# The last stage of a two-layer decoder: its weights loaded and split inside the stage before, its rows finished batch by batch

## Chip, cores and metric

One core of a Trainium2 chip runs the whole program in one launch. The metric is the device time of an execution in microseconds (us), lower is better.

## What is computed

The reference is a decoder of two layers on 8 sequences (batches) of 128 tokens with 512 features, every part followed by a residual add and a layernorm. The change touches the last two parts, a cross attention and a linear layer with routed low-rank adapters:

```python
x = _layernorm(x + _L1_xattn_ref(x, ctx, mask, Wq, Wk, Wv, Wo, q_norm_w, k_norm_w))   # 32 heads, 8 kv groups of 4, head size 128
q = x[:, 107:-1, :].mean(axis=1)
routing = softmax(q @ router_W.T + router_b)          # 8 experts
base = x @ W.T + b                                    # W: 512 x 512
t = einsum('bsd,erd->bser', x, A)                     # A: 8 experts x 16, 512
lora = einsum('bser,eor,be->bso', t, B, routing) * 2.0
x = _layernorm(x + base + lora)
```

All float32. A matmul to near float32 accuracy is made of three products in the type fp32r: each operand is split into a rounded high part and the low part left over, and high x high, low x high and high x low are accumulated (`three`, lines 69 to 73).

## The kernel before

`program` (line 2078) runs six stages one after the other. A stage owns its buffers, PSUM banks and semaphores; each engine has its own instruction stream in a stage, written out by hand, and engines meet only at semaphores. Between stages the semaphores are cleared and all engines meet at a barrier (lines 2096, 2097). No planner orders anything: the order of an engine's work is the order of the code. `m` holds what lives through all stages: x by token (`xtok`, token on the partition, batch, feature), x transposed and split (`xT_hi`, `xT_lo`), the context likewise, and small arrays of the layernorm.

**The second cross attention** (`cross1_stage`, line 873) works in 64 units, 8 groups of heads times 8 batches, unit u = 8 * group + batch. Its weights come group by group: SyncE loads raw q, k and v, and o weights (lines 912 to 930), each when the split of the group before has freed the raw buffer; GpSimd splits the next group while TensorE works on this one. A piece of the split is two GpSimd operations, a product with ones that gives the high part (line 937) and a subtract (line 939). A group has 2 pieces for k and v, 4 for q and 4 for o, spread over the eight steps of the group (lines 977 to 984): k and v in steps 0 and 1, q in steps 1 to 4, o in steps 4 to 7. In the same stream GpSimd multiplies the probabilities (line 972), takes the powers to -1/2 for the layernorm of finished batches (`batch_rstd`, line 1583, called from 976) and those of the q and k norm (line 989), which VectorE waits for in each unit. While the last group is worked on (units 56 to 63), the code before has nothing to split, and the layernorm of the stage runs batch by batch, from step 60 on: `batch_stats` (1572 to 1578) and `batch_scale` (1588) on VectorE, transposes on TensorE (1595), the split of the transposed x on ScalarE and VectorE (1601, 1606).

**The last stage** (`lora_stage`, line 1950). SyncE issues six loads: router weights and bias, the bias of the layer, A, W and B (lines 1982 to 1987). VectorE sums the high and low parts of x over the tokens 107 to 126 and forms q (2036 to 2039), casts W, A and B to the high part when all three have landed (2041, 2042), does the small steps of the router (2045 to 2050), copies the turned routing weights (2052), multiplies the product of x and A with them (2056) and splits the result (2057, 2059), adds the layer's bias to all of x in one operation (2060), and then adds each batch's rows from PSUM (2064). GpSimd takes the low parts of W, A and B (1997, 1998), for which it waits for the loads and for both casts. TensorE does the router's product (2006), the product of x and A for all batches in two banks of four batches each (24 products, 512 columns), turns the routing weights (2015), and then does the rows of each batch, 12 products with W and 3 with B into one of two banks, where batch b waits for VectorE's add of batch b - 2. When all rows are added, `norm_vector` (line 83) runs the statistics of all batches (86), their aggregates (89), one operation for the variances (91), and, after one power on GpSimd (106), the scaling of each batch (95). SyncE stores a batch when it is scaled (1990).

## Time and profile before

| what | value |
|---|---|
| median of 3 runs | 1765.85 us (1761.96 to 1769.78) |
| profiled execution | 1768.64 us |
| its span | 1766.8 us |
| TensorE busy, mean granted clock | 1557.7 us (88%), 0.936 |
| VectorE / ScalarE / GpSimd busy | 923.5 / 788.7 / 734.9 us |
| chain that ended last in the last stage begins | 1694.6 us |

The span runs from the first to the last instruction of the profiled execution. In the rows below, PE is TensorE's products, PEld its weight loads, DVE VectorE, ACT ScalarE, POOL GpSimd, SP SyncE; L2064 is line 2064 of the kernel. A timeline row gives the start and the duration in us, the engine, the line, what is written from what, the shapes, and how often (xN: a run of alike instructions put together, with their busy time in sum). In brackets stands how long the engine was idle before and what released it. Successive products overlap, so the distance from start to start is what one costs. A clock of 1.00 is 2.4 GHz, 0.50 is 1.2 GHz.

### The profile page before, as it was taken

What the parts mean: (1) busy time and instruction counts of PE and PEld (TensorE: products, weight loads), DVE (VectorE), ACT (ScalarE), POOL (GpSimd) and SP (SyncE); (2) the same over time, 40 slices, a digit from 0 to 9 for tenths busy, and PEclk for the clock granted to TensorE, in tenths of its full rate; (3) what the DMA queues carried; (4) which work ended last, traced back from release to release, by engine and by line L of the source; (5) the groups of instructions that cost most, each with busy time, mean ns of one, the idle gap of its engine ahead of it and who ended that gap; (6) DMA issues with size and microseconds to landing.
All of it is one profiled execution on the core that took longest, in us unless ns stands there. A gap on an engine that the chain in (4) does not pass through costs nothing. (4 is left out here: it accounts for less than half of the span.)

```text
span 1766.8 us, 28778 instructions
## 1 busy us (share of the span) xinstructions
PE 1557.7 (88%) x10647; PEld 1286.8 (73%) x10647; DVE 923.5 (52%) x1621; ACT 788.7 (45%) x2417; POOL 734.9 (42%) x589
## 2 busy tenths in 40 slices
PE   5888799999997699986999648999999999999836
PEld 3767497888885478875777437888888888888724
DVE  0627611333346588773567724555555555556644
ACT  2231223444443355534899714545545445445400
POOL 4100113444422599843533544555554555542210
PEclk9888899999999799998999859999999999999978
DMA  6100100100100643104000040101100110000011
GB/s 197 36 0 0 36 19 19 38 19 21 45 6 1 213 163 125 36 1 150 1 2 25 25 132 25 37 25 37 48 28 34 37 37 25 25 1 1 1 42 48
DMA packets 63474, 77.74 MB, mean 44 GB/s; under 512 B 13884, under 2 KB 43052, under 8 KB 63340
## 3 DMA queue, kind: packets, MB, share of 16 engines
q1 hardware_dynamic: 60860, 74.36, 13.3%
q8 instruction: 84, 1.38, 0.3%
q0 software_dynamic: 464, 1.32, 0.3%
q10 hardware_dynamic: 2016, 0.27, 0.1%
q14 instruction: 50, 0.41, 0.1%
HBM read 73.85 MB, written 2.10 MB: 43 GB/s over the span
## 5 line engine op out<-in xcount | busy, mean ns | idle before, releaser
L989 POOL TENSOR_TENSOR xa_rs<-xa_ms,minus_half 128x5 f32<-128x5 f32 x64 | 74.7, 1167 | 171.4 <-DVE xa_ms L1211 171.4
L972 POOL TENSOR_TENSOR xa_prob<-xa_prob,xa_inv 128x512 f32<-128x512 f32 x64 | 66.6, 1040 | 138.3 <-DVE xa_inv L1178 138.3
L605 POOL TENSOR_TENSOR xa_prob<-xa_prob,xa_inv 128x1024 f32<-128x1024 f32 x32 | 60.6, 1895 | 142.2 <-DVE xa_inv L859 142.2
L1156 ACT ACTIVATE xa_prob<-xa_prob,xa_peak 128x128 f32<-128x128 f32 x256 | 99.8, 391 | 42.5 <-DVE xa_peak L1222 42.5
L1206 DVE TENSOR_REDUCE xa_ssq<-xa_qn 128x4 f32<-128x512 f32 x64 | 43.9, 686 | 136.4 <-ACT xa_qn L1142 136.4
L1502 DVE SCALAR_TENSOR_TENSOR ff_acc<-ff_ring,ff_sT,ff_acc 128x512 f32<-128x512 f32 x140 | 100.4, 747 | 21.9 <-ACT ff_acc L1456 12.7
L71 PE MATMUL xa_qp<-xa_q_hi,xT_hi 128*128 128x512 f32 x256 | 108.0, 422 | 1.7 <-DVE xa_q_lo L1169 1.7
L1406 PE MATMUL ff_ring<-xT_hi,ff_w 128*128 128x512 f32 x224 | 93.0, 415 | 17.9 <-DVE ff_acc L1502 11.6
L71 PE MATMUL xa_rows<-xa_o_hi,xa_out_hi 128*128 128x512 f32 x256 | 101.6, 397 | 5.2 <-DVE xtok L1185 5.2
L1884 ACT ACTIVATE sa_work<-sa_work,sa_peak 128x128 f32<-128x128 f32 x256 | 99.1, 393 | 10.3 <-DVE sa_peak L1921 10.2
L72 PE MATMUL xa_qp<-xa_q_hi,xT_lo 128*128 128x512 f32 x256 | 102.4, 400 | 0.0
L73 PE MATMUL xa_rows<-xa_o_lo,xa_out_hi 128*128 128x512 f32 x256 | 102.2, 399 | 0.0
L73 PE MATMUL xa_qp<-xa_q_lo,xT_hi 128*128 128x512 f32 x256 | 102.0, 398 | 0.0
L1142 ACT ACTIVATE xa_qn<-xa_qp 128x512 f32<-128x512 f32 x64 | 38.2, 597 | 142.8 <-PE xa_qp L73 142.8
L72 PE MATMUL xa_rows<-xa_o_hi,xa_out_lo 128*128 128x512 f32 x256 | 101.6, 397 | 0.0
L1718 POOL TENSOR_TENSOR sa_work<-sa_work,sa_inv 128x1024 f32<-128x1024 f32 x32 | 60.7, 1898 | 93.9 <-DVE sa_inv L1925 93.7
L841 DVE TENSOR_REDUCE xa_peak<-xa_score 128x4 f32<-128x1024 f32 x32 | 39.1, 1223 | 115.6 <-PE xa_score L683 115.6
L1407 PE MATMUL ff_ring<-xT_lo,ff_w 128*128 128x512 f32 x224 | 91.7, 409 | 0.0
L71 PE MATMUL xa_kvp<-xa_kv_hi,cT_hi 128*128 128x256 f32 x256 | 78.8, 308 | 8.6 <-DVE xa_kv_lo L1164 8.6
L1456 ACT ACTIVATE ff_acc<-ff_ring,ff_sT 128x512 f32<-128x512 f32 x84 | 56.9, 685 | 49.8 <-PE ff_ring L1407 49.2
L73 PE MATMUL xa_kvp<-xa_kv_lo,cT_hi 128*128 128x256 f32 x256 | 73.3, 286 | 0.0
L72 PE MATMUL xa_kvp<-xa_kv_hi,cT_lo 128*128 128x256 f32 x256 | 73.1, 285 | 0.0
(390 smaller groups left out, 4820.9 us busy)
## 6 DMA issues: line engine op xcount, KB each, us to landing
xa_raw_q<-in_wq SPq DMA_DIRECT2D x8, 1024.0 KB, 5.4
xa_raw_o<-in_wo SPq DMA_DIRECT2D x8, 1024.0 KB, 5.3
ff_dn_q<-in_down_w SPq DMA_DIRECT2D x7, 512.0 KB, 3.5
ff_dn_z<-in_down_z SPq DMA_DIRECT2D x7, 512.0 KB, 5.1
ff_dn_s<-in_down_s SPq DMA_DIRECT2D x7, 512.0 KB, 6.5
pre<-in_wq SPq DMA_DIRECT2D x16, 192.0 KB, 3.3
pre<-in_wo SPq DMA_DIRECT2D x16, 192.0 KB, 3.7
sa_work<-in_w_qkvT SPq DMA_DIRECT2D x3, 1024.0 KB, 8.3
```

Source lines behind the costliest of these rows:

```text
L71: pe.matmul(out, a_hi, b_hi, start=first, stop=False)
L72: pe.matmul(out, a_lo, b_hi, start=False, stop=False)
L73: return pe.matmul(out, a_hi, b_lo, start=False, stop=last)
L605: pool.tensor_tensor(prob[:, t % 3, :, :], prob[:, t % 3, :, :], bc(inv[:, t % 3, :], 2, [P, Q, KEYS]), ALU.mult).then_inc(s["norm"], 1)
L972: pool.tensor_tensor(prob[:, u % 2, :, :], prob[:, u % 2, :, :], bc(inv[:, u % 2, :], 2, [P, Q, S]), ALU.mult).then_inc(s["norm"], 1)
L989: pool.tensor_tensor(rs[:, :], ms[:, :], m.minus_half[:, 0:Q + 1], ALU.pow).then_inc(s["rs"], 1)
L1156: last = act.activation(prob[:, u % 2, h, :], prob[:, u % 2, h, :], ACT.Exp, bias=peak[:, u % 2, h:h + 1], accum_out=total[:, u % 2, h:h + 1])
L1406: pe.matmul(bank[:, :], w[:, T % 3, c, a, f], m.xT_hi[:, c, cols], start=True, stop=False)
L1407: pe.matmul(bank[:, :], w[:, T % 3, c, a, f], m.xT_lo[:, c, cols], start=False, stop=True).then_inc(s["grp"], 1)
L1502: dve.scalar_tensor_tensor(acc[:, n % SETS, slot, :], ring[(8 * n + i) % RING][:, :], column(n, i), acc[:, n % SETS, slot, :], ALU.mult, A ...
L1718: pool.tensor_tensor(prob[:, u % 3, :, :], prob[:, u % 3, :, :], bc(inv[:, u % 3, :], 2, [P, HC, S]), ALU.mult).then_inc(s["norm"], 1)
L1884: last = act.activation(prob[:, t % 3, h, :], prob[:, t % 3, h, :], ACT.Exp, bias=peak[:, t % 3, h:h + 1], accum_out=total[:, t % 3, h:h + 1])
```

## The change

It adds a class `Late`, made once ahead of the cross attention and kept to the end, that holds the split q, kv and o weight buffers of that stage, the raw o buffer, the router's weights and bias, and, as a part of the raw o buffer, the layer's bias. The cross attention runs its load and split for a ninth "group": A takes the place of the k weights (128 columns), W that of q, B that of one piece of o. So SyncE issues the six loads there, behind the waits for the splits of group 7 and 8, and waits for the constants to land before it goes to the barrier; GpSimd splits 2 pieces of A (steps 56, 57, half the width), 4 of W (steps 57 to 60) and 1 of B (step 60).

In the last stage the loads, casts and subtracts are gone. GpSimd adds the layer's bias to x, one batch at a time, and then takes the power of one batch at a time. TensorE begins with the 12 products of x and W of batch 0, then does the router, x and A, the turn of the routing weights (into a bank of its own), and then the W products of batch b followed by the B products of batch b - 1. There are four banks for rows. The split of t is done in two halves of four batches, the high part on ScalarE. VectorE adds the rows of batch b, scales batch b - 1, and takes the statistics of batch b. SyncE's stores are as before, each behind its batch's scaling.

```diff
+class Late:
+
+
+    def __init__(self, sb):
+        self.q_hi, self.q_lo = (sb("late_" + n, [P, 2, KC, D], F32R) for n in ("q_hi", "q_lo"))
+        self.kv_hi, self.kv_lo = (sb("late_" + n, [P, 2, KC, 2 * P], F32R) for n in ("kv_hi", "kv_lo"))
+        self.o_hi, self.o_lo = (sb("late_" + n, [P, 2, KC, D], F32R) for n in ("o_hi", "o_lo"))
+        self.r_w, self.r_b = sb("late_r_w", [P, KC, B]), sb("late_r_b", [B, B])
+        self.raw_o = sb("late_raw_o", [P, KC, D])
+        self.bias = self.raw_o[:, 1, :]
...
-        raw_q, raw_kv, raw_o = sb("raw_q", [P, KC, QW]), sb("raw_kv", [P, KC, KW]), sb("raw_o", [P, Q, D])
-        q_hi, q_lo = (sb(n, [P, 2, KC, QW], F32R) for n in ("q_hi", "q_lo"))
-        kv_hi, kv_lo = (sb(n, [P, 2, KC, KW], F32R) for n in ("kv_hi", "kv_lo"))
-        o_hi, o_lo = (sb(n, [P, 2, Q, D], F32R) for n in ("o_hi", "o_lo"))
+        raw_q, raw_kv, raw_o = sb("raw_q", [P, KC, QW]), sb("raw_kv", [P, KC, KW]), m.late.raw_o
+        q_hi, q_lo, kv_hi, kv_lo, o_hi, o_lo = m.late.q_hi, m.late.q_lo, m.late.kv_hi, m.late.kv_lo, m.late.o_hi, m.late.o_lo
...
-                for g in range(G):
+                for g in range(G + 1):
                     if g == 1:
                         sp.wait_ge(s["kv0_lo"], 1)
                     elif g:
                         sp.wait_ge(s["split_kv"], PIECES_KV * (g - 1))
+                    if g == G:
+                        sp.dma_start(raw_kv[:, :, 0:HD], io["f_aT"].rearrange("(c p) n -> p c n", p=P)).then_inc(s["ld_kv"], 16)
+                        sp.dma_start(m.late.r_w[:, :, :], io["r_wT"].rearrange("(c p) n -> p c n", p=P)).then_inc(s["ld_kv"], 16)
+                        sp.dma_start(m.late.r_b[:, :], io["r_b"].partition_broadcast(B)).then_inc(s["ld_c"], 16)
+                        sp.wait_ge(s["split_q"], PIECES_Q * (g - 1))
+                        sp.dma_start(raw_q[:, :, :], io["f_wT"].rearrange("(c p) n -> p c n", p=P)).then_inc(s["ld_q"], 16)
+                        sp.wait_ge(s["split_o"], PIECES_O * g)
+                        sp.dma_start(raw_o[:, 0, :], io["f_bT"]).then_inc(s["ld_o"], 16)
+                        sp.dma_start(m.late.bias, io["f_b"].partition_broadcast(P)).then_inc(s["ld_c"], 16)
+                        sp.wait_ge(s["ld_c"], 80)
+                        break
                     for n, w in enumerate((wk, wv)):
                         sp.dma_start(raw_kv[:, :, n * HD:(n + 1) * HD], w[:, :, g * HD:(g + 1) * HD]).then_inc(s["ld_kv"], 16)
...
                     c = slice(2 * i, 2 * i + 2)
-                    split(raw_kv[:, c, :], kv_hi[:, g % 2, c, :], kv_lo[:, g % 2, c, :], s["split_kv"],
+                    cols = slice(0, HD if g == G else KW)
+                    split(raw_kv[:, c, cols], kv_hi[:, g % 2, c, cols], kv_lo[:, g % 2, c, cols], s["split_kv"],
                           PIECES_O + 10 * (g - 1) + i + 1)
...
                     if UNITS - B <= u:
                         batch_rstd(pool, m, n4, u % B)
                     g, b = t // B + 1, t % B
-                    if g < G:
+                    if g <= G:
                         if b < 2:
                             split_kv(g, b)
                         if 1 <= b < 5:
                             split_q(g, b - 1)
-                        if b >= 4:
+                        if b == 4 or b > 4 and g < G:
                             split_o(g, b - 4)
...
+        BANKS = 4
+        w_hi, w_lo = m.late.q_hi[:, 0, :, :], m.late.q_lo[:, 0, :, :]
+        a_hi, a_lo = m.late.kv_hi[:, 0, :, 0:P], m.late.kv_lo[:, 0, :, 0:P]
+        b_hi, b_lo = m.late.o_hi[:, 0, 0, :], m.late.o_lo[:, 0, 0, :]
...
-        rows = [pb(f"rows{i}") for i in range(2)]
-        small = pb("small")
+        rows = [pb(f"rows{i}") for i in range(BANKS)]
+        small, turned = pb("small"), pb("turned")
...
             def _(sp):
-                sp.dma_start(r_w[:, :, :], io["r_wT"].rearrange("(c p) n -> p c n", p=P)).then_inc(s["ld_s"], 16)
-                sp.dma_start(r_b[:, :], io["r_b"].partition_broadcast(B)).then_inc(s["ld_s"], 16)
-                sp.dma_start(bias[:, :], io["f_b"].partition_broadcast(P)).then_inc(s["ld_s"], 16)
-                sp.dma_start(w_raw[:, :, D:WA], io["f_aT"].rearrange("(c p) n -> p c n", p=P)).then_inc(s["ld_w"], 16)
-                sp.dma_start(w_raw[:, :, 0:D], io["f_wT"].rearrange("(c p) n -> p c n", p=P)).then_inc(s["ld_w"], 16)
-                sp.dma_start(b_raw[:, :], io["f_bT"]).then_inc(s["ld_w"], 16)
                 for b in range(B):
                     sp.wait_ge(n5["x"], b + 1)
                     sp.dma_start(io["out"][b, :, :], m.xtok[:, b, :]).then_inc(s["stored"], 16)
@@ -1992,41 +2005,49 @@
 
             @block.gpsimd
             def _(pool):
-                pool.wait_ge(s["ld_w"], 48)
-                pool.wait_ge(s["hi"], 2)
-                pool.tensor_tensor(w_lo[:, :, :], w_raw[:, :, :], raw(w_hi[:, :, :]), ALU.subtract).then_inc(s["lo"], 1)
-                pool.tensor_tensor(b_lo[:, :], b_raw[:, :], raw(b_hi[:, :]), ALU.subtract).then_inc(s["lo"], 1)
-                norm_gpsimd(pool, m, n5)
+                for b in range(B):
+                    pool.tensor_tensor(m.xtok[:, b, :], m.xtok[:, b, :], m.late.bias, ALU.add).then_inc(s["res"], 1)
+                for b in range(B):
+                    batch_rstd(pool, m, n5, b)
...
-                pe.wait_ge(s["ld_s"], 48)
+                def base(b):
+                    if b >= BANKS:
+                        pe.wait_ge(s["add"], b - BANKS + 1)
+                    for c in range(KC):
+                        three(pe, rows[b % BANKS][:, :], m.xT_hi[:, c, b * P:(b + 1) * P], m.xT_lo[:, c, b * P:(b + 1) * P],
+                              w_hi[:, c, :], w_lo[:, c, :], c == 0, False)
+
+                def adapted(b):
+                    pe.wait_ge(s["t_lo"], b // 4 + 1)
+                    three(pe, rows[b % BANKS][:, :], t_hi[:, b, :], t_lo[:, b, :], b_hi, b_lo, False, True).then_inc(s["rows"], 1)
+
+                base(0)
                 pe.wait_ge(s["q"], 1)
                 for c in range(KC):
-                    last = pe.matmul(small[0:B, 0:E_], q[:, c, :], r_w[:, c, :], start=c == 0, stop=c == KC - 1)
+                    last = pe.matmul(small[0:B, 0:E_], q[:, c, :], m.late.r_w[:, c, :], start=c == 0, stop=c == KC - 1)
                 last.then_inc(s["logits"], 1)
...
                 pe.wait_ge(s["wide"], 1)
-                pe.matmul(small[:, 64:64 + B], wide[:, :, :].rearrange("b e r -> b (e r)"), m.ident[0:B, 0:B], start=True, stop=True).then_inc(s["route"], 1)
...
-                pe.wait_ge(s["lo"], 2)
-                for b in range(B):
-                    if b >= 2:
-                        pe.wait_ge(s["add"], b - 1)
-                    for c in range(KC):
-                        three(pe, rows[b % 2][:, :], m.xT_hi[:, c, b * P:(b + 1) * P], m.xT_lo[:, c, b * P:(b + 1) * P],
-                              w_hi[:, c, 0:D], w_lo[:, c, 0:D], c == 0, False)
-                    pe.wait_ge(s["t_lo"], 1)
-                    three(pe, rows[b % 2][:, :], t_hi[:, b, :], t_lo[:, b, :], b_hi[:, :], b_lo[:, :], False, True).then_inc(s["rows"], 1)
+                pe.matmul(turned[:, 0:B], wide[:, :, :].rearrange("b e r -> b (e r)"), m.ident[0:B, 0:B], start=True, stop=True).then_inc(s["wide_T"], 1)
+                for b in range(1, B):
+                    base(b)
+                    adapted(b - 1)
+                adapted(B - 1)
...
                 act.wait_ge(s["lg"], 1)
                 act.activation(pr[:, :], lg[:, :], ACT.Exp, bias=pk[:, :], accum_out=tot[:, :]).then_inc(s["exp"], 1)
+                for n in range(2):
+                    bs = slice(4 * n, 4 * n + 4)
+                    act.wait_ge(s["t"], n + 1)
+                    act.activation(t_hi[:, bs, :], t[:, bs, :], ACT.Copy).then_inc(s["t_hi"], 1)
...
                 dve.tensor_scalar(q[:, :, :], q[:, :, :], 1.0 / (Q_END - Q_FIRST), None, ALU.mult).then_inc(s["q"], 1)
-                dve.wait_ge(s["ld_w"], 48)
-                dve.tensor_copy(w_hi[:, :, :], w_raw[:, :, :]).then_inc(s["hi"], 1)
-                dve.tensor_copy(b_hi[:, :], b_raw[:, :]).then_inc(s["hi"], 1)
-                dve.wait_ge(s["ld_s"], 48)
                 dve.wait_ge(s["logits"], 1)
...
-                dve.wait_ge(s["route"], 1)
-                ch.step(dve.tensor_copy(route[:, :], small[:, 64:64 + B]))
-                dve.wait_ge(s["low"], 2)
+                dve.wait_ge(s["wide_T"], 1)
+                ch.step(dve.tensor_copy(route[:, :], turned[:, 0:B]))
                 for n in range(2):
                     bs = slice(4 * n, 4 * n + 4)
-                    ch.step(dve.tensor_tensor(t[:, bs, :], low[n][:, :].rearrange("p (b s) -> p b s", b=4), bc(route[:, bs], 2, [P, 4, S]), ALU.mult))
-                dve.tensor_copy(t_hi[:, :, :], t[:, :, :]).then_inc(s["t_hi"], 1)
-                dve.wait_ge(s["t_hi"], 1)
-                dve.tensor_tensor(t_lo[:, :, :], t[:, :, :], raw(t_hi[:, :, :]), ALU.subtract).then_inc(s["t_lo"], 1)
-                dve.tensor_tensor(m.xtok[:, :, :], m.xtok[:, :, :], bc(bias[:, :], 1, [P, B, D]), ALU.add).then_inc(s["res"], 1)
-                dve.wait_ge(s["res"], 1)
+                    dve.wait_ge(s["low"], n + 1)
+                    dve.tensor_tensor(t[:, bs, :], low[n][:, :].rearrange("p (b s) -> p b s", b=4), bc(route[:, bs], 2, [P, 4, S]),
+                                      ALU.mult).then_inc(s["t"], 1)
+                for n in range(2):
+                    bs = slice(4 * n, 4 * n + 4)
+                    dve.wait_ge(s["t_hi"], n + 1)
+                    dve.tensor_tensor(t_lo[:, bs, :], t[:, bs, :], raw(t_hi[:, bs, :]), ALU.subtract).then_inc(s["t_lo"], 1)
                 for b in range(B):
                     dve.wait_ge(s["rows"], b + 1)
-                    dve.tensor_tensor(m.xtok[:, b, :], m.xtok[:, b, :], rows[b % 2][:, :], ALU.add).then_inc(s["add"], 1)
-                dve.wait_ge(s["add"], B)
-                norm_vector(dve, m, n5, transposed=False)
+                    dve.wait_ge(s["res"], b + 1)
+                    dve.tensor_tensor(m.xtok[:, b, :], m.xtok[:, b, :], rows[b % BANKS][:, :], ALU.add).then_inc(s["add"], 1)
+                    if b:
+                        batch_scale(dve, m, n5, b - 1)
+                    dve.wait_ge(s["add"], b + 1)
+                    batch_stats(dve, m, n5, b)
+                batch_scale(dve, m, n5, B - 1)
...
+            if n == SHARED:
+                m.late = Late(sb)
```

## Rows read from the trace of the kernel before

**Rows 1.** By stretch: busy us (count) of PE, PEld, DVE, ACT, POOL; clock; DMA.
```profile
1591.00:1629.00 38.00, 38.00 (x226) 33.02 (x225) 22.90 (x49) 18.97 (x64) 9.38 (x9) 1.00 0.00 1
...
1694.00:1713.00 19.00, 0.36 (x8) 0.25 (x8) 8.74 (x10) 0.39 (x2) 5.27 (x1) 0.50 0.33 97
...
1716.00:1718.00 2.00, 2.00 (x10) 1.59 (x9) 0.00 (x0) 0.00 (x0) 0.00 (x0) 0.94 0.00 0
```

**Rows 2.** Timeline of VectorE and GpSimd: the last stage's load and split.
```profile
1705.75 1.49 DVE L2041 CAST lo_w_hi<-lo_w_raw 128x2560 fp32r<-128x2560 f32 x1 [8.93 <-DMA lo_b_raw<-in_f_bT]
...
1707.73 5.57 POOL L1997 TENSOR_TENSOR lo_w_lo<-lo_w_raw,lo_w_hi 128x2560 fp32r<-128x2560 f32 x1 [16.79 <-DVE lo_b_hi L2042]
1713.26 1.27 POOL L1998 TENSOR_TENSOR lo_b_lo<-lo_b_raw,lo_b_hi 128x512 fp32r<-128x512 f32 x1
```

**Rows 3.** Timeline of TensorE in the last stage.
```profile
1713.35 0.79 PE L71 MATMUL lo_low<-xT_hi,lo_w_hi 128*128 128x512 f32 x1 [12.45 <-POOL lo_w_lo L1997]
...
1720.38 0.38 PE L2015 MATMUL lo_small<-ident,lo_wide 8*128 8x8 f32 x2
...
1733.12 0.39 PE L71 MATMUL lo_rows<-lo_w_hi,xT_hi 128*128 128x512 f32 x1
...
1750.38 0.39 PE L73 MATMUL lo_rows<-lo_b_lo,lo_t_hi 128*128 128x512 f32 x1
```

**Rows 4.** Timeline of VectorE at the end, and the view of line 1990.
```profile
1751.54 4.84 DVE L86 BATCH_NORM_STATS2 stats<-xtok 128x6 f32<-128x512 f32 x8
...
1759.02 3.74 DVE L95 TENSOR_SCALAR xtok<-xtok,meanvar,rstd 128x512 f32<-128x512 f32 x8 [1.76 <-POOL rstd L106]
...
L1990 SPq DMA_DIRECT2D out<-xtok x8: 360/502/647, 1759.6 to 1763.4; - x8
```

**Rows 5.** Timeline of VectorE and ScalarE: router's mean, adapter, a copy.
```profile
1694.71 0.82 DVE L2036 TENSOR_REDUCE lo_q_hi<-xT_hi 128x32 f32<-128x640 f32 x1 [1.06 <-PEq L2097]
...
1696.64 0.18 DVE L2039 TENSOR_SCALAR lo_q<-lo_q 128x32 f32<-128x32 f32 x1
...
1720.80 0.17 DVE L2052 COPY lo_route<-lo_small 128x8 f32<-128x8 f32 x1 [6.20 <-PE lo_small L2015]
1721.00 1.42 DVE L2056 TENSOR_TENSOR lo_t<-lo_low,lo_route 128x512 f32<-128x512 f32 x2
...
1692.33 0.60 ACT L1601 ACTIVATE xT_hi<-xa_kt 128x512 fp32r<-128x512 f32 x1 [4.47 <-PE xa_kt L1595]
```

**Rows 6.** Timeline of TensorE at the lower clock, units of the cross attention's end.
```profile
1673.46 0.76 PE L71 MATMUL xa_rows<-xa_o_hi,xa_out_hi 128*128 128x512 f32 x1 [3.11 <-DVE xtok L1185]
...
1678.29 0.59 PE L73 MATMUL xa_rows<-xa_o_lo,xa_out_hi 128*128 128x512 f32 x1
```

**Rows 7.** Timeline of VectorE: a batch's add, variance and scaling, cross attention.
```profile
1688.50 0.68 DVE L1185 TENSOR_TENSOR xtok<-xtok,xa_rows 128x512 f32<-128x512 f32 x1
...
1690.16 0.15 DVE L1578 TENSOR_SCALAR var<-meanvar 128x1 f32<-128x1 f32 x1
1690.97 0.55 DVE L1588 TENSOR_SCALAR xtok<-xtok,meanvar,rstd 128x512 f32<-128x512 f32 x1 [0.66 <-POOL rstd L1583]
```

**Rows 8.** Timeline of VectorE, last stage: an 8x8 scaling, the bias add.
```profile
1708.47 4.85 DVE L2049 TENSOR_SCALAR lo_pr<-lo_pr,lo_inv 8x8 f32<-8x8 f32 x1
...
1724.32 4.42 DVE L2060 TENSOR_TENSOR xtok<-xtok,lo_bias 128x4096 f32<-128x4096 f32 x1
```

**Rows 9.** Timeline of GpSimd and VectorE in the cross attention, units 52 and 60.
```profile
1547.69 1.04 POOL L937 TENSOR_TENSOR xa_q_hi<-xa_raw_q,ones 128x512 fp32r<-128x512 f32 x1
...
1552.99 1.17 POOL L989 TENSOR_TENSOR xa_rs<-xa_ms,minus_half 128x5 f32<-128x5 f32 x1 [0.54 <-DVE xa_ms L1211]
...
1624.57 0.56 POOL L1583 TENSOR_TENSOR rstd<-var,minus_half 128x1 f32<-128x1 f32 x1 [0.68 <-DVE var L1578]
1629.16 1.17 POOL L989 TENSOR_TENSOR xa_rs<-xa_ms,minus_half 128x5 f32<-128x5 f32 x1 [4.03 <-DVE xa_ms L1211]
...
1630.91 0.68 DVE L1231 TENSOR_TENSOR xa_qn<-xa_qp,xa_rs 128x512 f32<-128x512 f32 x1
```

More of the change, by code:

```diff
@@ L1971, in lora_stage @@
         low = [pb(f"low{i}") for i in range(2)]
-        rows = [pb(f"rows{i}") for i in range(2)]
-        small = pb("small")
+        rows = [pb(f"rows{i}") for i in range(BANKS)]
+        small, turned = pb("small"), pb("turned")
         s = {n: sem("lo_" + n) for n in (
-            "ld_w", "ld_s", "hi", "lo", "chain", "q", "logits", "lg", "exp", "wide", "route", "low", "t_hi",
-            "t_lo", "res", "rows", "add", "stored")}
+            "chain", "q", "logits", "lg", "exp", "wide", "wide_T", "route", "low", "t", "t_hi", "t_lo", "res", "rows", "add", "stored")}
         n5 = norm_sems(sem, "n5")
@@ L2072 @@
 PREFETCHED = 3
+SHARED = 4
 def program(nc, io):
```

11 lines of the change are left out of this document (2 added, 9 removed).

## The prediction

> **What bounds the kernel now.** I read the stage's own stretches first, since busy shares over 1766.8 us say nothing of a change in the last 72. In the stretches by window [rows 1] TensorE is busy without a gap in the second cross attention before its last layernorms (38.00 of 38 us, clock 1.00), and in the first 19 us of the last stage it does 0.36 us of work at a clock of 0.50. The VectorE and GpSimd rows of that gap [rows 2] say why: VectorE's cast (1.49 us) begins at 1705.75, after 8.93 us idle that a load ended; behind it come GpSimd's subtract (5.57) and TensorE's first long product at 1713.35 [rows 3]. From there to the last product (1750.38, over at 1750.77) the engine is the bound, apart from two stops of under 1 us. Behind it VectorE does all eight batches' statistics, then the scaling, then SyncE's stores, to the end at 1766.8 [rows 4]. So of the stage's 72 us, from 1694.7, 18.6 are load and split, 37.4 TensorE, 16.0 a tail in which TensorE is idle. The change takes up the first and the last.
>
> **Part 1, the load and split leave.** After the barrier TensorE may start at once with batch 0's 12 products of x and W, at about 1694.75 (VectorE starts at 1694.71, [rows 5]). It was idle before, so it starts at the lower clock, 0.50 or 1.2 GHz, where 11 steps from one product to the next took 4.83 us [rows 6], 0.43 us each without the slow first; at 2.4 GHz a step is 17.26/74 = 0.233 us from 1733.12 to 1750.38 [rows 3]. The stretch of rows 6 stayed low for all its 12 products; in the old last stage, begun at 1713.35, the clock is 0.94 from 1716 on [rows 1], so some six were slow. I take nine, midway: 9 x 0.43 + 3 x 0.233 = 4.6, so 1699.3; bounds 2.8 (none slow) and 5.1.
> The mean x for the router needs two reductions, an add and a scaling, over at 1696.8 before [rows 5], so it is ready while TensorE works on batch 0. Router products: 0.36 us (TensorE's whole work in the second stretch of [rows 1]) and 0.1 of handover, 1699.8. Then 24 products of x and A, 24 x 0.233 = 5.6, 1705.4. The turn of the routing weights took 0.38 [rows 3]: 1705.8. Then 7 x 12 + 8 x 3 = 108 products at 0.233, 25.2 us, no stop between: last result at 1731.1, batch 6's at 1730.4.
> Why no stop: four banks instead of two remove the wait on VectorE's add. The wait for the adapter's t_lo is covered now: the routing copy starts, as before, 0.42 after the turn did (1720.80 after 1720.38, [rows 5, 3]), so at 1705.8; the two products of t take 0.71 each from 0.20 later, ScalarE's copy of the first half (0.60, the nearest row is its copy of the same size, [rows 5]) lies beside the second, and a half's subtract is as long as such a product, 0.71: t_lo of batches 0 to 3 at about 1708.2, while batch 1's products end at 1708.6. Margin 0.4 us; if it is missed, the price is the overshoot, under 1 us.
>
> **Part 2, the tail batch by batch.** VectorE's work for a batch is 1.66 from the add's start to the variance's, 0.15 for that, and a scaling 0.47 (3.74/8) [rows 7, 4]: 2.3 us against 15 x 0.233 = 3.5 us of TensorE, so VectorE keeps up until batch 7, which comes 0.7 us after batch 6. From batch 6's rows at 1730.45: add and statistics 1.66 with scale(5) between, 0.47; variance 0.15; add and statistics of batch 7, 1.66, with scale(6) between, 0.47 (its power on GpSimd lies beside the add: variance to scaling is 0.81, [rows 7]); variance to scaling 0.81; scaling 0.55: 5.8 us, 1736.2. The last store costs what it did: its issue started at 1763.4 and the span ended at 1766.8 [rows 4], 3.4 us. The stores before it are 3.5 us apart but for the last, against some 0.5 us of issue, so SyncE is free. End: 1739.7, or 27.1 us earlier.
>
> **Part 3, what moves to GpSimd in the last stage.** The bias add was 4.42 us on VectorE [rows 8], beside TensorE. Eight adds of one batch at 1.27 (the 128x512 subtract, [rows 2]) keep GpSimd busy from 1694.7 to 1704.9; the first row add is at about 1710, so they are hidden, and would cost nothing up to 5 us more. But there is a collision: VectorE's 8x8 scaling took 4.85 us, where the 128x32 one of q took 0.18 [rows 5], while GpSimd's subtract ran, and ended as that ended [rows 8, 2]. The same kind of instruction in the new order (the scaling of q, of the probabilities, and the widening copy) can each wait for one add of 1.27. q: from 1696.8 to at most 1698.1, still ahead of 1699.3. Probabilities and copy: 1699.8, five small steps before them at about 0.2 (as q's, [rows 5]), then 2 x 1.4 of waiting and work: 1703.6, ahead of 1705.4. Cost zero as long as TensorE has those products; without that cover 4 us.
> The Trainium skill, SBUF — State Buffer, section "Who interferes with whom", says GpSimd and a two-port VectorE instruction lock each other out for a whole instruction, and that a VectorE instruction with two SBUF inputs also contends with GpSimd's reads. The trace agrees with the first clause (the 4.85 us); no row of this case shows a pair of the second kind. By it q's add would wait as well, and q would come at 1699.3 at the latest: nothing against the sum above, but 1.7 us if the 12 products run at the higher clock and end at 1697.6. It is also why E, below, stays at 0.04: one wait would last no longer than one add.
>
> **Part 4, the ninth group in the cross attention.** SyncE's loads of it wait for the splits of group 7 and land long before they are used; SyncE has nothing else queued there. The splits of w are five GpSimd steps, units 56 to 60, like those of the groups before, where the stage ran at full speed. Split steps with four operations end 0.54 us before the mean square arrives (unit 52, the first two of [rows 9]). New is unit 60: there GpSimd first waits for the layernorm's variance and does its power from 1624.57 to 1625.12, and only then the last q piece and the one o piece. The four took 1552.45 - 1547.69 = 4.76 us, so 1629.9, where the unit's own power began at 1629.16: 0.75 late. VectorE used its result at 1630.91, against 1630.33 when it was there, so 0.2 us of the 0.75 is exposed, up to 0.7 if the layernorm's scaling (0.55, [rows 7]) holds GpSimd up first. TensorE has no slack there (38.00 of 38 us, [rows 1]), so all of it counts: I take 0.5, bounds 0 and 2 (other units hit also). Other steps: nothing, under the same cover; without it the whole split would be exposed, 5 pieces at 4.76/2 and two of A at half of that, 14 us.
>
> **The sum.** -27.1 + 0.5 = -26.6 us. The profiled execution took 1768.64 us, 1.84 over its span: 1742.0 by that. It lies 2.8 over the median of the runs, 1765.85, so the forecast for the median is 1739.2. Some 0.5% (9 us) is what a measurement of this kernel tells from no change; this is three times that.
>
> **Rivals.**
> A, the forecast, 0.76: TensorE bounds the stage from the barrier on.
> B, the clock stays low longer, 0.10: if both the first 12 products and the 24 of x and A run at 1.2 GHz, 27 more slow steps x 0.2 = +5.3 us, 1744.5. For it: the 0.50 of [rows 1] and the idle before. Against: both earlier recoveries were over within 12 products.
> C, the ninth group is exposed, 0.09: GpSimd's splits in units 56 to 60 hold up their powers by their whole length, 14 us, 1752.7. For it: unit 60's four pieces have no room. Against: the 0.54 us that remain with the same load in unit 52.
> D, slower, 0.01: the same place tips the clock. If a GpSimd delay makes TensorE stand over about 3 us in each unit (it fell to 0.50 after 3.11 us of standing in [rows 6]), the units run at 1.2 GHz: TensorE's 10 us of a unit become up to 20, and eight units cost up to 80 us against the 27 gained. It decides from three such units (3 x 10 against 27). Against it: the largest delay I can work out is 0.75 us.
> E, the stage is not freed, 0.04: t_lo or the router is late after all (GpSimd's adds hold VectorE for all 10 us, and q comes at 1705): +5.5 us on TensorE's path, 1744.7, or with the clock lost again 1747. For it: the 4.85 us. Against: the copy behind it got through as soon as its one GpSimd instruction ended.
> **How the numbers follow.** Low: none slow, unit 60 free, and a median 4 us lower (the three runs lie 4 either side): 1732. High: B and E with that scatter, and C where half of it is exposed: 1751; what is left out is the rest of C, D and stray medians, under 2 in 10. Faster by over 0.5% (below 1757) in A, B, E, nearly all of C: 0.96; within 0.5%: 0.03; slower: 0.01.
>
> **What the next profile should show.** TensorE's first product of the last stage within 0.2 us of VectorE's first instruction; no idle before the adapter's products or the row products; 108 products at 0.233; scalings between adds; eight stores 3.5 us apart but the last; last product to end of span about 8.7 us (now 16.0); unit 60's power 0.75 us late and every other where it was. The forecast is wrong if the last product starts later than 37 us behind the barrier, if q or the routing turn is what TensorE waits for, or if the cross attention grows by over 2 us.

## The result and the profile after

| what | before | after |
|---|---|---|
| median | 1767.57 us (1761.96 to 1769.78, 4 runs) | 1742.91 us (1742.37 to 1745.53, 4 runs) |
| profiled execution, its span | 1768.64, 1766.8 us | 1745.53, 1743.7 us |
| mean granted clock of TensorE | 0.936 | 0.943 |
| last stage: first instruction to end of span | 1694.71 to 1766.8, 72.1 us | 1699.49 to 1743.7, 44.2 us |

The ratio is 0.9868 with an interval of 0.9841 to 0.9895: 24.7 us faster, where 26.6 were forecast.

TensorE in the changed last stage (timeline), which answers to [rows 3]:

```profile
1699.49 0.77 PE L83 MATMUL lo_rows<-late_q_hi,xT_hi 128*128 128x512 f32 x1 [2.41 <-PEq L2121]
...
1704.62 0.35 PE L2029 MATMUL lo_small<-late_r_w,lo_q 128*8 128x8 f32 x8
...
1710.61 0.38 PE L2037 MATMUL lo_turned<-ident,lo_wide 8*128 8x8 f32 x2
...
1713.83 0.39 PE L83 MATMUL lo_rows<-late_o_hi,lo_t_hi 128*128 128x512 f32 x1
...
1735.99 0.39 PE L85 MATMUL lo_rows<-late_o_lo,lo_t_hi 128*128 128x512 f32 x1
```

Only the first row has a bracket, the barrier. The router, the turn and the first adapter product start without a stop. Where TensorE stood for 12.45 us before [rows 3], it now works; its last product is issued 36.5 us behind the start of the stage. The end of VectorE's stream and the view of the stores, which answer to [rows 4]:

```profile
1735.73 0.69 DVE L2082 TENSOR_TENSOR xtok<-xtok,lo_rows 128x512 f32<-128x512 f32 x1 [1.34 <-PE lo_rows L85]
...
1738.54 0.55 DVE L1610 TENSOR_SCALAR xtok<-xtok,meanvar,rstd 128x512 f32<-128x512 f32 x1
...
1740.76 0.55 DVE L1610 TENSOR_SCALAR xtok<-xtok,meanvar,rstd 128x512 f32<-128x512 f32 x1 [0.66 <-POOL rstd L1605]
```
```profile
L2003 SPq DMA_DIRECT2D out<-xtok x8: 332/332/348, 1719.4 to 1741.3; - x8
```

Batch 6's rows are added at 1735.73, batch 7 is scaled 5.6 us later, and the last store is issued at 1741.3. An issue takes 332 ns at the median, where the eight in a burst took 502 [rows 4].

The small steps on VectorE, and GpSimd beside them, which answer to [rows 5, 8]:

```profile
1701.20 0.84 DVE L2059 TENSOR_TENSOR lo_q<-lo_q_hi,lo_q_lo 128x32 f32<-128x32 f32 x1
1702.08 1.20 DVE L2060 TENSOR_SCALAR lo_q<-lo_q 128x32 f32<-128x32 f32 x1
...
1705.99 0.99 DVE L2066 TENSOR_SCALAR lo_pr<-lo_pr,lo_inv 8x8 f32<-8x8 f32 x1
1707.02 1.28 DVE L2067 COPY lo_wide<-lo_pr 8x128 f32<-8x128 f32 x1
```
```profile
1699.47 10.00 POOL L2009 TENSOR_TENSOR xtok<-xtok,late_raw_o 128x512 f32<-128x512 f32 x8 [4.21 <-POOLq L2121]
```

The scaling of q took 0.18 us with GpSimd idle [rows 5] and takes 1.20 beside its adds. With GpSimd idle the four take 0.19, 0.18, 0.22 and 0.21 us (e4, below), so all four are stretched, and none reaches TensorE.

So the stage is 0.7 us shorter than the 44.95 of the forecast, yet the span ends at 1743.7 against the forecast's 1740.2: the stage **starts** later. The forecast put it 0.5 behind 1694.71; it is 4.8 behind. The interval from one power of the q and k norm to that eight units on gives the place:

| stretch, us | before | after |
|---|---|---|
| up to the first of these powers | 1053.71 | 1056.60 |
| first eight units | 80.41 | 78.55 |
| each of the next six eights | 76.16 | 76.43 |
| units 57 to 63, together | 67.91 | 68.84 |
| of these, unit 60 | 9.53 | 10.41 |
| last power to the start of the last stage | 35.73 | 36.94 |

The first two lines are scatter, +1.0 in sum: over the executions profiled for this study they run from 1050.2 to 1057.9 and from 78.0 to 80.7, whatever the kernel. The others are to be explained: +1.6 for the six eights, +0.9 for units 57 to 63 and +1.2 for the last stretch, 3.7 in all.

### The profile page after: what moved, and what is told of

The parts are those of the page before. It is cut to its first block and busy times, and to the rows that moved or that the text cites. A ratio compares the mean times of both kernels' runs of the same rounds, so it can differ in the third digit from the quotient of the medians.

```text
span 1743.7 us, 28819 instructions
## 1 busy us (share of the span) xinstructions
PE 1555.7 (89%) x10647; PEld 1284.7 (74%) x10647; DVE 916.8 (53%) x1625; ACT 789.6 (45%) x2419; POOL 755.0 (43%) x616
## 5 line engine op out<-in xcount | busy, mean ns | idle before, releaser
L1178 ACT ACTIVATE xa_prob<-xa_prob,xa_peak 128x128 f32<-128x128 f32 x256 | 99.9, 392 | 42.9 <-DVE xa_peak L1244 42.9
L1524 DVE SCALAR_TENSOR_TENSOR ff_acc<-ff_ring,ff_sT,ff_acc 128x512 f32<-128x512 f32 x140 | 100.4, 747 | 21.9 <-ACT ff_acc L1478 11.9
L83 PE MATMUL xa_rows<-late_o_hi,xa_out_hi 128*128 128x512 f32 x256 | 104.1, 406 | 5.2 <-DVE xtok L1207 5.2
L83 PE MATMUL xa_qp<-late_q_hi,xT_hi 128*128 128x512 f32 x256 | 106.8, 417 | 2.0 <-DVE late_q_lo L1191 2.0
L85 PE MATMUL xa_rows<-late_o_lo,xa_out_hi 128*128 128x512 f32 x256 | 102.0, 398 | 0.0
L84 PE MATMUL xa_rows<-late_o_hi,xa_out_lo 128*128 128x512 f32 x256 | 101.5, 397 | 0.0
L85 PE MATMUL xa_qp<-late_q_lo,xT_hi 128*128 128x512 f32 x256 | 101.2, 395 | 0.0
L84 PE MATMUL xa_qp<-late_q_hi,xT_lo 128*128 128x512 f32 x256 | 101.1, 395 | 0.0
L853 DVE TENSOR_REDUCE xa_peak<-xa_score 128x4 f32<-128x1024 f32 x32 | 39.1, 1223 | 115.7 <-PE xa_score L695 115.7
L83 PE MATMUL xa_kvp<-late_kv_hi,cT_hi 128*128 128x256 f32 x256 | 78.6, 307 | 8.6 <-DVE late_kv_lo L1186 8.6
L1605 POOL TENSOR_TENSOR rstd<-var,minus_half 128x1 f32<-128x1 f32 x40 | 23.4, 586 | 114.6 <-DVE var L1600 114.5
L84 PE MATMUL xa_kvp<-late_kv_hi,cT_lo 128*128 128x256 f32 x256 | 72.7, 284 | 0.0
```

The lines of the kernel that those rows point to most:

```text
L83: pe.matmul(out, a_hi, b_hi, start=first, stop=False)
L84: pe.matmul(out, a_lo, b_hi, start=False, stop=False)
L85: return pe.matmul(out, a_hi, b_lo, start=False, stop=last)
L1178: last = act.activation(prob[:, u % 2, h, :], prob[:, u % 2, h, :], ACT.Exp, bias=peak[:, u % 2, h:h + 1], accum_out=total[:, u % 2, h:h + 1])
L1524: dve.scalar_tensor_tensor(acc[:, n % SETS, slot, :], ring[(8 * n + i) % RING][:, :], column(n, i), acc[:, n % SETS, slot, :], ALU.mult, A ...
```

## The experiments

Each edit is made to the changed kernel, unless said otherwise. Kernels named together ran on one chip and share the runs of the kernel before.

### First four: the two halves, and GpSimd's hold on VectorE

The kernel before: 1768.3 us (14 runs).

**e1_early_only** keeps the ninth group and puts the old order of the last stage behind it (two banks, bias add on VectorE, norm at the end):

```diff
-                base(0)
                 pe.wait_ge(s["q"], 1)
...
-                    pool.tensor_tensor(m.xtok[:, b, :], m.xtok[:, b, :], m.late.bias, ALU.add).then_inc(s["res"], 1)
-                    batch_rstd(pool, m, n5, b)
+                norm_gpsimd(pool, m, n5)
...
+                norm_vector(dve, m, n5, transposed=False)
```

> Only the ninth group stays; the last stage runs in its old order (product of x and A first, two banks, bias add on VectorE, all statistics behind the last row add). Theory, the two halves add up: TensorE's first long product comes right behind q, some 2.5 us after the barrier instead of 18.6, so the stage takes about 72 - 16 = 56 us and the kernel gains 15 us. Rival, the early start is worth little because TensorE then waits for the router or for VectorE's bias add: the stage takes over 65 us.

Measured: 1754.8 us, ratio 0.9925 [0.9899, 0.9951], 13.5 us faster. The stage took 57.4 us. TensorE stood until q was there, and the norm came in one block again:

```profile
1699.19 0.36 PE L2015 MATMUL lo_small<-late_r_w,lo_q 128*8 128x8 f32 x8 [4.58 <-DVE lo_q L2046]
...
1739.02 4.85 DVE L98 BATCH_NORM_STATS2 stats<-xtok 128x6 f32<-128x512 f32 x8
```

**e2_batch_only** is the kernel before with the new order, banks and batch-wise tail; loads and split stay in the last stage. The excerpt is against the changed kernel:

```diff
+                pool.wait_ge(s["ld_w"], 48)
+                pool.wait_ge(s["hi"], 2)
+                pool.tensor_tensor(w_lo[:, :, :], w_raw[:, :, :], raw(w_hi[:, :, :]), ALU.subtract).then_inc(s["lo"], 1)
+                pool.tensor_tensor(b_lo[:, :], b_raw[:, :], raw(b_hi[:, :]), ALU.subtract).then_inc(s["lo"], 1)
...
-                base(0)
                 pe.wait_ge(s["q"], 1)
...
+                pe.wait_ge(s["lo"], 2)
+                base(0)
```

> Only the new order of the last stage; its weights are loaded and split in the stage as before, with batch 0's products behind the split. Theory: first long product again 18.6 us behind the barrier, no stops behind it (1.6 us less) and a tail of 7.3 instead of 16.0 us: the stage takes about 62 us, the kernel gains 10. With the 15 of the other half that makes 25 of the 27 of the stage; the 2 left over are the router's q, which is hidden only if TensorE has weights to work with. Rival, the tail is overlap that the early weights made possible: the gain here is under 5 us.

Measured: 1762.99 us, ratio 0.9961 [0.9947, 0.9976], 5.3 us faster. The stage took 64.1 us, 8.0 less than before, against 62 expected. Part of the miss is my edit, in which batch 0 waits for the low part of B as well as for that of W, one subtract of 1.26 us more:

```profile
1718.48 1.26 POOL L1999 TENSOR_TENSOR lo_b_lo<-lo_b_raw,lo_b_hi 128x512 fp32r<-128x512 f32 x1
```
```profile
1719.80 0.80 PE L71 MATMUL lo_rows<-lo_w_hi,xT_hi 128*128 128x512 f32 x1 [13.93 <-POOL lo_b_lo L1999]
```

The rest lies at the clock: 13 products run at the lower one behind this wait, six in the kernel before. The interval for the kernel's gain, 4.2 to 9.4 us, holds the 8.0 of the stage.

What follows: in the stage the halves give 14.7 and 8.0 of the 27.9 us. Together they are 5 us short of the whole, and all of that lies between the barrier and the last product; the tails, 16.5 and 7.7 us, are those of the old and the new order. Three things make up most of it, by the starts of the products:

- 2.2 us in which TensorE stands for q behind the barrier in e1_early_only, with no batch 0 to work on (the 4.58 of the bracket begin before the barrier).
- 1.1 us by which the first long product is later in e2_batch_only than before (19.8 us into the stage, 18.6 before), which is my edit's wait.
- About 1.5 us of slow products: 13 in each half's run against 6 before and 11 in the changed kernel.

So only the first of the three, under half of the 5 us, is what the halves do for each other.

**e3_bias_one** makes one GpSimd instruction of the eight bias adds:

```diff
-                for b in range(B):
-                    pool.tensor_tensor(m.xtok[:, b, :], m.xtok[:, b, :], m.late.bias, ALU.add).then_inc(s["res"], 1)
+                pool.tensor_tensor(m.xtok[:, :, :], m.xtok[:, :, :], bc(m.late.bias, 1, [P, B, D]), ALU.add).then_inc(s["res"], B)
```

> GpSimd's eight bias adds are one instruction of 4096 columns, about 10 us. Theory (VectorE is shut out for a whole GpSimd instruction): q's add, two inputs in SBUF, and its scaling end only with it, some 10 us behind the barrier; TensorE stops about 5 us behind batch 0's products, and the stage takes 49 to 51.5 us instead of 44.2. Rival (VectorE gets through between): q within 4 us, stage at 44.2.

Measured in one run: 1748.59 us; the stage took 50.8 us (44.2 with eight adds). VectorE, GpSimd and the wait:

```profile
1697.67 7.22 DVE L2058 TENSOR_TENSOR lo_q<-lo_q_hi,lo_q_lo 128x32 f32<-128x32 f32 x1
1704.92 0.18 DVE L2059 TENSOR_SCALAR lo_q<-lo_q 128x32 f32<-128x32 f32 x1
```
```profile
1695.94 8.90 POOL L2008 TENSOR_TENSOR xtok<-xtok,late_raw_o 128x4096 f32<-128x4096 f32 x1 [4.21 <-POOLq L2120]
```
```profile
PE lo_small L2028 <- DVE lo_q L2059: 4.1, 1, 4.1
```

The add of q's halves, an instruction with two inputs in SBUF, ends with GpSimd's instruction (1704.89 and 1704.84), and the scaling behind it is back at 0.18. TensorE stands 4.1 us and comes back with twelve products at the lower clock (0.43 apart). That is rival E's mechanism: +6.6 us in the stage, where the prediction had 5.5, or 7.8 with the clock lost again. The reductions in front (0.82 each in every kernel) are not held. The Trainium skill, SBUF — State Buffer, "Who interferes with whom", has both clauses: the pair of ports is held for a whole instruction, and two SBUF inputs on VectorE contend with GpSimd's reads. The kernel before showed the first alone; this run shows the second, 0.19 becoming 7.22 us, held until GpSimd's instruction ended.

**e4_bias_late** lets the bias adds wait until the routing weights are widened:

```diff
+                pool.wait_ge(s["wide"], 1)
                 for b in range(B):
                     pool.tensor_tensor(m.xtok[:, b, :], m.xtok[:, b, :], m.late.bias, ALU.add).then_inc(s["res"], 1)
```

> GpSimd's eight bias adds wait for the widened routing weights. Theory: q's add and scaling and the router's scaling and copy fall back to 0.2 us each, the router ends 3 us earlier, and the stage stays at 44.2 us since TensorE was busy over all of it; now the low part of t, two inputs in SBUF, runs beside GpSimd and may take 1.3 us longer, for a stop of TensorE of 0 to 1 us. Rival 1: the waits of VectorE were on the path, the stage gets 1 us or more shorter. Rival 2: two inputs in SBUF don't collide, the low part of t stays at 0.69 us a half.

Measured in one run: 1742.2 us; the stage took 44.2 us as in the changed kernel. The scaling of q is short again, and the hold goes on to the low half of t, 1.23 us each instead of 0.65:

```profile
1698.10 0.18 DVE L2061 TENSOR_SCALAR lo_q<-lo_q 128x32 f32<-128x32 f32 x1
...
1709.29 2.46 DVE L2079 TENSOR_TENSOR lo_t_lo<-lo_t,lo_t_hi 128x512 fp32r<-128x512 f32 x2
```

So the holds on q and on the probabilities cost this kernel nothing, as Part 3 said: their removal buys nothing.

### Next four: what the cross attention and the tail lose

The kernel before: 1767.83 us (9 runs).

**e9_pad96** puts an unused buffer of 96 bytes per partition behind `r_b`. The program places `xa_out_hi`, the attention output that these products hold stationary, at byte 219456 before, 219616 after and 219712 here; the first and the last are multiples of 64, the one after the change is not.

```diff
+        self.pad = sb("late_pad", [P, 24])
         self.raw_o = sb("late_raw_o", [P, KC, D])
```

> The changed kernel with one unused buffer of 96 bytes a partition behind the router's weights, so that the cross attention's own buffers lie 256 bytes further than in the kernel before instead of 160; nothing else. In every kernel with the shared weight buffers a group of eight units takes 76.43 us, without them 76.16, and the 0.27 lie in the products of the output rows (2.80 us for 12 instead of 2.77). Theory: the cause is where the stationary operand starts (160 is no multiple of 64, 256 is): groups go back to 76.16 and the kernel is 2.1 us faster than the changed one. Rival: it is the moved weights or their distance from the rest: 76.43 stays.

Measured: 1738.52 us, ratio 0.9827 [0.9813, 0.9841]. Each of the six eights takes 76.16 us again, unit 60 still 10.42. By the view of lines from 1200 to 1580 us (groups: busy us, mean ns of one; same shape and count; the granted clock of this window is 1.00 in both), the three products of the output rows in the changed kernel and then in this one:

```profile
L83 PE MATMUL xa_rows<-late_o_hi,xa_out_hi 128*128 128x512 f32 x160 | 63.8, 399 | 0.0
L85 PE MATMUL xa_rows<-late_o_lo,xa_out_hi 128*128 128x512 f32 x160 | 63.0, 394 | 0.0
L84 PE MATMUL xa_rows<-late_o_hi,xa_out_lo 128*128 128x512 f32 x160 | 62.7, 392 | 0.0
```
```profile
L86 PE MATMUL xa_rows<-late_o_lo,xa_out_hi 128*128 128x512 f32 x160 | 63.2, 395 | 0.0
L85 PE MATMUL xa_rows<-late_o_hi,xa_out_lo 128*128 128x512 f32 x160 | 63.0, 394 | 0.0
L84 PE MATMUL xa_rows<-late_o_hi,xa_out_hi 128*128 128x512 f32 x160 | 62.5, 390 | 0.0
```

The kernel before has 391, 394 and 396 for high x high, `late_o_hi` x `xa_out_lo` and `late_o_lo` x `xa_out_hi`. `late_o_hi` and `late_o_lo` lie ahead of the pad and did not move, `xa_out_hi` and `xa_out_lo` did, and so did every other buffer behind the pad. From start to start, the block of 12 products (four of each kind) takes 2.77 us before and 2.80 after: 0.03 of each unit, most of the 0.27 per eight. In all that is some 7 x 0.27 = 1.9 us.

So a shift of the buffers costs the time, and it isn't the moved weights. But it is not that every product with a shifted stationary operand slows: of the three kinds, one is 9 ns longer and the other two are 1 to 2 ns shorter, though one of these also holds `xa_out_hi` stationary, and `xa_out_lo` (4096 bytes behind it) is shifted by as much. Why it is that one is open. The median moved by more (the ratio is 0.0032 under that of the changed kernel measured again, below, on another chip, which is 5.7 us); only 1.9 of that is located here, and 1.2 more in the end of the stage, where this execution took 35.71 us instead of 36.94.

**e5_o_later** moves the piece of o from step 60 to 61:

```diff
-                        if b == 4 or b > 4 and g < G:
+                        if g < G and b >= 4:
                             split_o(g, b - 4)
+                        if g == G and b == 5:
+                            split_o(g, 0)
```

> The one o piece of the ninth group is split in step 61 instead of 60. Theory: unit 60 took 10.41 us (power to power) instead of 9.53 because GpSimd had the variance's wait and four split operations in it; with two it takes 9.5 to 9.6, unit 61, where GpSimd idled 4.07 us, keeps its 9.8 to 10.0, and the stage starts 0.8 us earlier. Rival: the delay comes from the layernorm's scaling being locked out by the q piece, which stays: 10.2 or more.

GpSimd in unit 60, the changed kernel and then this one:

```profile
1627.32 0.56 POOL L1605 TENSOR_TENSOR rstd<-var,minus_half 128x1 f32<-128x1 f32 x1 [0.68 <-DVE var L1600]
...
1631.39 1.28 POOL L960 TENSOR_TENSOR late_o_lo<-late_raw_o,late_o_hi 128x512 fp32r<-128x512 f32 x1
1632.79 1.17 POOL L1011 TENSOR_TENSOR xa_rs<-xa_ms,minus_half 128x5 f32<-128x5 f32 x1
```
```profile
1627.17 1.35 POOL L960 TENSOR_TENSOR late_q_lo<-xa_raw_q,late_q_hi 128x512 fp32r<-128x512 f32 x1
1630.14 1.17 POOL L1013 TENSOR_TENSOR xa_rs<-xa_ms,minus_half 128x5 f32<-128x5 f32 x1 [1.62 <-DVE xa_ms L1235]
```

In the changed kernel the unit's power comes straight behind the fourth split operation; with two operations it waits 1.62 us for VectorE. Unit 60 takes 9.55 instead of 10.41, unit 61 9.99 instead of 9.77: 0.64 us net. The run, 1743.46 us, says nothing at that size; the intervals do.

**e6_filler** issues 35 products whose result nobody reads, into a free bank, where TensorE stands at the end of the cross attention (10 and 6 before the rows of the last two units, 14 and 5 around the last transposes):

```diff
+                def fill(n):
+                    for _ in range(n):
+                        pe.matmul(qp[:, :], q_hi[:, 1, 0, 0:P], q_hi[:, 1, 1, :], start=True, stop=True)
...
                 values(UNITS - 2)
+                fill(10)
                 out_rows(UNITS - 2)
...
                 values(UNITS - 1)
+                fill(6)
                 out_rows(UNITS - 1)
                 turn_batch(UNITS - 2)
+                fill(14)
                 turn_batch(UNITS - 1)
+                fill(5)
```

> 35 products whose result nobody reads are put into the waits of TensorE at the end of the cross attention (10, 6, 14 and 5), so that it does not stand still there. Theory: the clock stays at 1.00 over the end of the stage and the start of the next; the 15 slow products of the cross attention's end, the slow transposes and the ten slow ones of the last stage cost 0.43 us no longer; from unit 63's power to the last stage 33.5 us instead of 36.9, the last stage 42.1 instead of 44.2: 5 us faster than the changed kernel. Rival: the clock falls all the same, or the fillers hold up what is behind them: within 1 us of the changed kernel.

Measured: 1737.71 us, ratio 0.9824 [0.981, 0.9838]. The stretch before the last stage, from 2.5 us behind unit 63's power on, by window (busy us and counts of PE, PEld, DVE, ACT, POOL; clock; DMA), in the changed kernel and then here:

```profile
1665.00:1699.40 34.40, 19.54 (x83) 14.64 (x81) 16.30 (x34) 7.54 (x22) 4.29 (x6) 0.82 0.00 1
```
```profile
1662.00:1693.00 31.00, 24.07 (x118) 18.40 (x116) 16.23 (x35) 7.45 (x22) 4.36 (x7) 1.00 0.00 1
```

The clock is 1.00 instead of 0.82, and the stretch from power to stage is 33.5 us instead of 36.9. In the last stage the 12 products of batch 0 run at full clock too (0.233 apart from the second on), but the stage is only 1.3 us shorter, 42.9 against 42.1 expected, and the row shows why:

```profile
1696.79 0.35 PE L2037 MATMUL lo_small<-late_r_w,lo_q 128*8 128x8 f32 x8 [0.79 <-DVE lo_q L2068]
```

TensorE is now ahead of q. It is the cover that Part 3 named: with the 12 products at the higher clock, GpSimd's hold on VectorE is exposed, 0.79 us of it.

**e7_no_lag** puts the B products of batches 1 to 7 right behind their own W products:

```diff
-                for b in range(1, B):
+                base(1)
+                adapted(0)
+                adapted(1)
+                for b in range(2, B):
                     base(b)
-                    adapted(b - 1)
-                adapted(B - 1)
+                    adapted(b)
```

> From batch 1 on a batch's adapter products come right behind its own W products, no longer behind those of the next batch, so batch 6 is ready 3.5 us ahead of batch 7 instead of 0.7. Theory: the end was VectorE's chain from batch 6's rows on (add, scaling, statistics of 6, then 7); now only batch 7's own is left, from the last product's start to the end 5.8 us instead of 7.7, and the stage takes 42.3 instead of 44.2. Rival: batch 7's own chain and the last store were the bound already: under 0.5 us.

The last two batches are 3.5 us apart instead of 0.7, so VectorE is done with batch 6 when the last rows come:

```profile
1734.62 0.69 DVE L2084 TENSOR_TENSOR xtok<-xtok,lo_rows 128x512 f32<-128x512 f32 x1 [1.34 <-PE lo_rows L85]
```

From the last product's start to the end it is 6.2 us instead of 7.7 (5.8 expected), and the stage 42.9 instead of 44.2. The median, 1743.11 us, does not show it: in this execution 24 products of the cross attention's end ran at the lower clock instead of 14, and the stretch before the stage took 39.2 us instead of 36.9.

### Last four: the changed kernel again, and all of it together

The kernel before: 1770.57 us (9 runs).

**e13_changed_again** is the changed kernel, unaltered, to compare with on the same chip.

> The changed kernel itself, on the same chip as the next three: 1741 to 1745 us, a group of units 76.43 us, the last stage 44.2 us; its start may lie 2 us either way, since TensorE's clock at the end of the cross attention comes back earlier or later from one execution to the next.

1745.13 us, ratio 0.9859 [0.9844, 0.9874]; stage 44.1, eights 76.43, unit 60 10.40.

**e12_pad32** pads by 32 bytes instead of 96 (`sb("late_pad", [P, 8])`), which puts `xa_out_hi` at 219648, a multiple of 64 too.

> The unused buffer has 32 bytes instead of 96, so the cross attention's own buffers lie 192 bytes further than in the kernel before. Theory, a stationary operand that starts at a multiple of 64 bytes is enough: groups take 76.16 us. Rival, it must be the old place to 128 or 256 bytes: 76.43.

1737.24 us in one run, the eights at 76.11: the third place on a multiple of 64 is no slower than the other two. It is even 0.05 quicker, where eights of one kernel differ by 0.01, so a multiple of 64 doesn't say all of it; and the only place off such a multiple is that of the changed kernel.

**e11_fill_bias_q** is the kernel with the fillers, and the bias adds wait for q:

```diff
+                pool.wait_ge(s["q"], 1)
                 for b in range(B):
                     pool.tensor_tensor(m.xtok[:, b, :], m.xtok[:, b, :], m.late.bias, ALU.add).then_inc(s["res"], 1)
```

> The unread products, and GpSimd's bias adds wait for q. Theory: with the clock at 1.00 batch 0's products no longer cover q, whose add and scaling wait for GpSimd's adds; TensorE stood 0.79 us for it. With the adds behind q that stop is gone, q is ready 2.1 us into the stage, and the stage takes 42.1 instead of 42.9 us. Rival: GpSimd's adds now collide with the low part of t, and the 0.8 come back there.

1739.09 us in one run; the stage is still 42.9 us. The stop before the router is gone, and VectorE's split of t now takes the hold:

```profile
1697.39 0.35 PE L2038 MATMUL lo_small<-late_r_w,lo_q 128*8 128x8 f32 x8
```
```profile
1705.40 2.40 DVE L2087 TENSOR_TENSOR lo_t_lo<-lo_t,lo_t_hi 128x512 fp32r<-128x512 f32 x2
```

```profile
1707.26 0.50 PE L83 MATMUL lo_rows<-late_o_hi,lo_t_hi 128*128 128x512 f32 x1 [0.49 <-DVE lo_t_lo L2087]
```

The first B product starts 0.89 us after the W product before it, where 0.23 is the pace. So the gain of 0.8 us before the router is lost at `t_lo`. The margin of 0.4 us that Part 1 gave this wait is as thin as it said.

**e10_together** has the pad of 96 bytes, the o piece in step 61, the fillers, the bias adds behind q, and no lag.

> The changed kernel with the 96 bytes, the o piece in step 61, the 35 unread products, the adapter products without lag, and GpSimd's bias adds behind q. Theory, the parts add up: 2.1 + 0.6 + 5 + 1.3 + 0.8 = 9.8 us less than the changed kernel, 1733 us. Rival, they overlap (the slow clock's loss and the others stand in the same waits): 1736 or more.

1733.25 us (1729.58 to 1735.62, 5 runs), ratio 0.9786 [0.9772, 0.9799]: 11.9 us under the changed kernel on the same chip, where 9.8 were expected. Against that kernel's profiled execution the trace gives 1.6 for the six eights, 0.9 for units 57 to 63, 3.5 before the stage and 2.8 in it (41.3 us), 8.8 in all; the medians differ by 3 us more than these two executions do, and that much the trace of one can't place. One stop is left:

```profile
1705.32 0.50 PE L84 MATMUL lo_rows<-late_o_hi,lo_t_hi 128*128 128x512 f32 x1 [0.47 <-DVE lo_t_lo L2092]
```

## Why the prediction was right, and what it missed

**Sign, mechanism and size hold.** The forecast was 1739.2 in 1732 to 1751, and 1742.91 was measured. In the trace the sum was 1740.2 for the span and 1743.7 came. The difference of 3.5 us is +4.3 before the stage (1.0 of it scatter ahead of the second eight units) and -0.75 in it.

**One of its own signs of being wrong came.** The prediction called itself wrong if the cross attention grew by over 2 us. From the second eight units on it grew by 3.7 us in this execution, or 2.5 without the last stretch. The change's gain comes out near the forecast because that loss is small beside the 27.9 us of the last stage, not because the loss was foreseen.

**Part 1, right.** TensorE starts at the barrier, no stop follows. Slow products were taken as nine; there were eleven (steps of 0.56, nine of 0.43, one of 0.40), and the router starts 5.1 us behind the start instead of 4.65. From the stage's start to batch 6's add it is 36.2 us against 35.7, and that is the difference. The t_lo wait was covered, and e10 and e11 show how nearly.

**Part 2, right but for one term.** From batch 6's add to the last scaling's end: 5.6 us against 5.8. The last store was put at 3.4 us, from its issue in the old kernel; it is 2.4 here. The old row was the eighth of a burst of issues, this one goes into an idle queue. The 1.0 us is the term mis-sized, and it made up for the slow products, which was luck.

**Part 3, right.** The holds are there, on both kinds of instruction, and cost nothing under batch 0's products (e4). The conditions it set are borne out: without the cover, or with one long instruction for eight short ones, they reach TensorE (e6, e3). Splitting the add by batch is what keeps a hold at one add, about 1.2 us.

**Part 4, too cheap.** Unit 60's four operations were seen; 0.5 was taken within 0 to 2. It is 0.86 in that unit, some 0.2 of which unit 61 gives back; e5 takes back 0.64.

**"Other steps: nothing" failed.** That sentence costed the ninth group's instructions in the other units and rightly found none exposed. But a second thing in the change reaches every unit: class `Late` moves the stage's buffers from `mask` on by 160 bytes, and the 12 products of a unit's output rows take 2.80 instead of 2.77 us, some 1.9 us over the stage (e9, e12). The prediction had no term for where buffers lie.

**The rest is the clock, and not wholly settled.** The stretch between the last power and the stage took 36.9 us instead of 35.7, and 39.2 in e7, by how many of its products ran at the lower clock: 14 in the changed kernel, 12 before, 24 in e7. It was 35.7 to 36.0 us in three executions with the aligned placement (before, e9, e12) and 36.8 to 37.1 in six with the other, but also 39.1 in e2, which is aligned, and 39.2 in e7, which isn't. So the pad may or may not reach it. What is shown is its price: with the waits filled, 33.3 to 33.5 in all three executions.

**The rivals.** B (clock low through 36 products) didn't come: eleven slow ones. C and D didn't come: 0.9 us over units 57 to 63, and TensorE stays at 1.00 there. E didn't come here, but e3 made it, at +6.6 us.

## What to carry to other kernels

Work that an idle engine can do one stage earlier pays in full only if the later stage has something to run from its first instant: with the weights early but the old order, TensorE still stood 2.2 us for q. When a change adds buffers, compare the time of units that it doesn't touch: a shift of addresses is an edit as well. And take a moved wait for settled only when the next consumer has been looked at: each hold taken off q turned up at the split of t.

## What the runs showed of the hardware

- With the stage's buffers shifted by 160 bytes, so that the stationary operands `xa_out_hi` and `xa_out_lo` start 32 bytes off a multiple of 64, a block of 12 fp32r products takes 2.80 us instead of 2.77, and eight units 76.43 instead of 76.16, at the same clock of 1.00. Two further places, both multiples of 64, gave 76.16 (e9) and 76.11 (e12). One of the three kinds of product carries it, 399 ns against 390.
- A two-input VectorE add of 128x32 was held 7.22 us by one GpSimd instruction of 8.90 us, but only 0.84 us by eight of about 1.25 that follow one another without a gap: VectorE gets in between two of them.
- A store issued into an idle queue was over 2.4 us after its issue began (2.0 to 2.1 from issue to landing for all eight), the last of a burst of eight 3.4 us (2.1 to 3.0).
- Behind one and the same wait of TensorE (3.11 us), 6 to 12 products ran at the lower clock, from one execution to the next (e13 6, the changed kernel 7, the kernel before 12).
- 35 unread products in waits of TensorE lift the mean granted clock of the cross attention's end from 0.82 to 1.00, and shorten it by 3.4 us though they add work.
